# Softmax scores from two 12-bit float32r parts on four row tiles, with the maximum subtracted by a second matmul

## The reference

```
qkv = x @ qkv_w.T + qkv_b                       # x: 2048 x 128, normalised
q, k, v = split(qkv), 16 heads of 8
scores = einsum('bhqe,bhke->bhqk', q, k) / sqrt(8)
attn = softmax(scores, axis=-1)
out = einsum('bhqk,bhke->bhqe', attn, v)
out = out @ proj_w.T + proj_b
```

## Time and profile before

| | |
|---|---|
| median of the runs | 1883.54 us |
| the profiled execution's span | 1880.9 us |
| PE busy | 1635.9 us (87%), 7285 instructions |
| DVE busy | 1354.7 us (72%) |
| ACT busy | 836.9 us (44%) |
| POOL busy | 222.4 us (12%) |
| DMA moved | 29.49 MB |
| softmax attention, two passes | about 218 to 1036 us |

### The profile page before, as it was taken

One profiled execution on the slowest core, in us unless ns is written; L12 is line 12 of the kernel. 1 busy time (PEld: TensorE's weight loads), 2 busy tenths in 40 slices (PEclk: granted clock), 3 DMA queues, 4 the chain that ended last, 5 costly groups with the idle time before them and its releaser, 6 DMA issues. The chain is left out here.

```text
span 1880.9 us, 23731 instructions
## 1 busy us (share of the span) xinstructions
PE 1635.9 (87%) x7285; PEld 683.8 (36%) x7285; DVE 1354.7 (72%) x1951; ACT 836.9 (44%) x1493; POOL 222.4 (12%) x145
## 2 busy tenths in 40 slices
PE   6987589999999999999998798899994356589999
PEld 3433112222222222222221443366661122256665
DVE  5776788888888778888880577666656999745654
ACT  2433427777676666667778253322223000042222
POOL 2222300000000000000000022211101324301110
PEclk8998659999999999999999899899996777799999
DMA  6000400011001100111000000000000000000000
GB/s 168 2 0 1 135 16 8 14 27 40 9 14 28 30 12 7 27 30 24 2 2 2 1 1 0 1 1 0 0 1 0 0 0 1 0 1 6 6 5 7
DMA packets 32021, 29.49 MB, mean 16 GB/s; under 512 B 7788, under 2 KB 27032, under 8 KB 31928
## 3 DMA queue, kind: packets, MB, share of 16 engines
q1 hardware_dynamic: 31928, 28.31, 5.9%
HBM read 22.13 MB, written 4.19 MB: 14 GB/s over the span
## 5 line engine op out<-in xcount | busy, mean ns | idle before, releaser
L1382 DVE TENSOR_REDUCE mx<-ps 128x1 f32<-128x1024 f32 x512 | 605.2, 1220 | 147.5 <-PE ps L1269 143.2
L1269 PE MATMUL ps<-k,q 72*128 72x512 bf16 x1024 | 403.0, 408 | 11.4 <-DVE mx L1382 9.3
L1304 PE MATMUL ps<-q,k 84*128 84x512 bf16 x1024 | 346.8, 384 | 20.7 <-ACT xn L1359 14.5
L1359 ACT ACTIVATE xT<-ps 128x512 f32<-128x512 f32 x512 | 265.1, 603 | 156.7 <-PE ps L1304 156.6
L1359 ACT ACTIVATE xn<-ps 128x512 f32<-128x512 f32 x512 | 266.2, 603 | 107.4 <-PE ps L1304 107.4
L1269 PEld LDWEIGHTS ps<-k,q 72*128 72x128 bf16 x1024 | 110.1, 115 | 331.4 <-DVE mx L1382 185.4
L854 ACT ACTIVATE silu<-ps 128x512 f32<-128x512 f32 x144 | 85.3, 596 | 265.3 <-PE ps L827 261.9
L1304 PEld LDWEIGHTS ps<-q,k 84*128 84x128 bf16 x1024 | 102.3, 102 | 185.6 <-ACT xn L1359 69.6
L889 DVE TENSOR_TENSOR hid<-ps,silu 128x512 f32<-128x512 f32 x144 | 97.8, 690 | 91.2 <-PE ps L831 89.6
L827 PE MATMUL ps<-xT,ew 128*128 (+1 forms) x288 | 151.0, 606 | 6.5 <-PEq L1750 4.8
L817 PEld LDWEIGHTS ps<-ew,hid 128*128 128x128 f32 x1152 | 138.7, 192 | 30.6 <-issue 29.9
(11 more groups left out here) (239 smaller groups left out, 1688.9 us busy)
## 6 DMA issues: line engine op xcount, KB each, us to landing
k<-k_parts SPq DMA_DIRECT2D x90, 64.0 KB
q<-q_parts SPq DMA_DIRECT2D x144, 32.0 KB
k<-k_parts SPq DMA_DIRECT2D x108, 32.0 KB
ew<-in_L_ffn_w_dram SPq DMA_DIRECT2D x2, 1024.0 KB
wraw<-in_L_ffn_w_dram SPq DMA_DIRECT2D x3, 512.0 KB, 6.7
q_parts<-part SPq DMA_DIRECT2D x4, 384.0 KB, 5.3
k_parts<-part SPq DMA_DIRECT2D x4, 384.0 KB, 2.6
v<-values SPq DMA_DIRECT2D x8, 144.0 KB, 4.2
```

What stands on the lines that cost most here:

```text
L1269: mm = nc.tensor.matmul(m.ps[:, S1B[i % 4], :], queries, k1[:, h, kc * CHUNK:(kc + 1) * CHUNK], start=True, stop=True)
L1304: nc.tensor.matmul(m.ps[:, S2_BANK[s], :], k2[:, h, kt * P:(kt + 1) * P], q[:, qc, h, :], start=True, stop=True).then_inc(s2_ready, 1)
L1359: nc.scalar.activation(ex[kt % P_RING][:, h, :], m.ps[:, S2_BANK[s], :], ACT.Exp).then_inc(exped, 1)
L1382: nc.vector.reduce_max(mx[:, h, qt, kc:kc + 1], m.ps[:, 2 * (i % 2):2 * (i % 2) + 2, :], AX.XY)\
```

## The change

q and k are split into two parts of 12 significant bits each, both held as 32-bit values: DVE cuts off the low 12 bits (`HI_BITS`), POOL subtracts to get the rest. Scores are formed from them by float32r matmuls over 2 x 2 x 8 = 32 rows, one head on each of four row tiles of 32 rows (partitions 0, 32, 64 and 96), so that a tile q or k1 or k2 holds all four heads of a group in 128 partitions. The rows of k no longer hold ones; a second matmul, over two rows of `ones` against the two parts of the negated maximum (`neg_row`), accumulates into the same bank after the score.

The first pass issues two matmuls together, of heads 0 and 1 or 2 and 3, on two row tiles and into two banks; the DVE reduction then gives one maximum for each of two heads and not one over two banks. There are 32 such pairs a unit, over key blocks in the outer loop. The second pass forms scores 0 and 1, then subtracts both maxima, and the same for 2 and 3. Each load of q, k1 or k2 is four DMAs of 32 partitions (every fourth), in place of nine of eight; the maxima are eight DMAs of two by four runs in place of four. Parts in DRAM are float32, two of them. The first group's k1 and the first q also come directly from the part tile, not from DRAM. ACT's fill of the ones in k2 is gone, and DVE's split of the maximum has two steps in place of five.

```
+PARTS2 = 2
+ROW_TILE = 32
+ROW_BLOCKS = PARTS2 * PARTS2
+HI_BITS = -4096
...
-    dram_q = nc.dram_tensor("q_parts", [PARTS, D, T], BF16, kind="Internal").ap()
-    dram_k = nc.dram_tensor("k_parts", [PARTS, D, T], BF16, kind="Internal").ap()
+    dram_q = nc.dram_tensor("q_parts", [PARTS2, D, T], F32, kind="Internal").ap()
+    dram_k = nc.dram_tensor("k_parts", [PARTS2, D, T], F32, kind="Internal").ap()
...
-    q = m.sb("q", [ROWS_M, CHUNKS, GH, CHUNK], BF16, stack=kv_stack)
-    k1 = m.sb("k1", [ROWS, GH, T], BF16, stack=kv_stack)
-    neg_part = m.sb("neg_part", [P, TPC, 32], BF16, stack=kv_stack)
+    q = m.sb("q", [P, CHUNKS, CHUNK], F32R, stack=kv_stack)
+    k1 = m.sb("k1", [P, T], F32R, stack=kv_stack)
+    ones = m.sb("ones", [P, P], F32R, stack=kv_stack)
+    neg_part = m.sb("neg_part", [P, TPC, 32], stack=kv_stack)
...
+    def rows_of(tile, r):
+        return tile[r:P:ROW_BLOCKS, :].bitcast(F32)
...
+            def low_part(n):
+                pool.wait_ge(hi_ready, n + 1)
+                nc.gpsimd.tensor_tensor(part[:, n % PART_RING, 1, :], full[:, n % 2, :], part[:, n % PART_RING, 0, :],
+                                        ALU.subtract).then_inc(lo_ready, 1)
...
-                step(nc.vector.tensor_tensor(rest[:, :], full[:, n % 2, :], part[:, n % PART_RING, 0, :], ALU.subtract))
-                step(nc.vector.tensor_copy(part[:, n % PART_RING, 1, :], rest[:, :]))
-                nc.vector.tensor_tensor(part[:, n % PART_RING, 2, :], rest[:, :], part[:, n % PART_RING, 1, :], ALU.subtract)\
-                    .then_inc(parts_ready, 1)
-                dve.wait_ge(parts_ready, n + 1)
+                dve.wait_ge(f32_ready, n + 1)
+                part_free(dve, n)
+                nc.vector.tensor_scalar(part[:, n % PART_RING, 0, :].bitcast(I32), full[:, n % 2, :].bitcast(I32), HI_BITS,
+                                        None, ALU.bitwise_and).then_inc(hi_ready, 1)
...
+                if n < N_DIRECT:
+                    tile = q[:, 0, :] if s == 0 else k1[:, c * CHUNK:(c + 1) * CHUNK]
+                    for r in range(ROW_BLOCKS):
+                        i = r // PARTS2 if s == 0 else r % PARTS2
+                        sp.dma_start(rows_of(tile, r), part[0:GH * HD, slot, i, :]).then_inc(direct[slot], 16)
...
-        k2 = m.sb("k2", [ROWS_M, GH, T], BF16, stack=stack)
+        k2 = m.sb("k2", [P, T], F32R, stack=stack)
...
-        done = [max(0, (k + 1 - HOLE) * STEPS // (STEPS - HOLE)) for k in range(-1, STEPS)]
+        done = [max(0, (k + 1 - HOLE) * PAIRS // (STEPS - HOLE)) for k in range(-1, STEPS)]
...
+            for r in range(ROW_BLOCKS):
+                eng.dma_start(rows_of(q[:, qc, :], r),
+                              dram_q[r // PARTS2, bass.ts(g, GH * HD), qc * CHUNK:(qc + 1) * CHUNK]).then_inc(q_loaded[qc], 16)
...
                 for b in range(P // 32):
-                    rows = neg_turned[b * 32:b * 32 + PARTS * GH, :, :].rearrange("r j t -> r (j t)").unsqueeze(1)\
-                        .to_broadcast([PARTS * GH, GH, P])
-                    sp.dma_start(q[ROWS:ROWS_M, qc, :, b * P:(b + 1) * P], rows).then_inc(max_loaded, 16)
+                    for i in range(PARTS2):
+                        rows = slice(b * 32 + i * GH, b * 32 + (i + 1) * GH)
+                        sp.dma_start(neg_row[i:P:ROW_TILE, slot, b * P:(b + 1) * P].bitcast(F32),
+                                     neg_turned[rows, :, :].rearrange("h j t -> h (j t)")).then_inc(max_loaded, 16)
 
...
-                h, qt, kc = i // (TPC * CHUNKS), i // CHUNKS % TPC, i % CHUNKS
...
-                if i % 2 == 0 and not (isinstance(g, int) and g == 0 and qc == 0 and i < len(S1B)):
-                    pe.wait_ge(s1_used, (g * CHUNKS + qc) * PAIRS + (i // 2 - 1))
-                queries = q[0:ROWS, qc, h, :].rearrange("r (p t) -> r t p", t=TPC)[:, qt, :]
-                mm = nc.tensor.matmul(m.ps[:, S1B[i % 4], :], queries,
-                                      k1[:, h, kc * CHUNK:(kc + 1) * CHUNK], start=True, stop=True)
-                if i % 2 == 1:
-                    mm.then_inc(s1_ready, 1)
+                    pe.wait_ge(q_loaded[qc], DMAS_R * g)
+                if qc == 0 and i % (PAIRS // CHUNKS) == 0 and not (isinstance(g, int) and g == 0):
+                    pe.wait_ge(k1_loaded[kc], DMAS_R * g)
+                if not (isinstance(g, int) and g == 0 and qc == 0 and i < 2):
+                    pe.wait_ge(s1_used, (g * CHUNKS + qc) * PAIRS + (i - 1))
+                for h in (2 * pair, 2 * pair + 1):
+                    rows = slice(h * ROW_TILE, (h + 1) * ROW_TILE)
+                    queries = q[rows, qc, :].rearrange("r (p t) -> r t p", t=TPC)[:, qt, :]
+                    mm = nc.tensor.matmul(m.ps[:, S1B[h], :], queries, k1[rows, kc * CHUNK:(kc + 1) * CHUNK],
+                                          start=True, stop=True)
+                mm.then_inc(s1_ready, 1)
...
-                def score(s):
-                    kt, h = s // GH, s % GH
-                    if not (first and s < len(S2B)):
-                        pe.wait_ge(exped, u * STEPS + (s - S2_SINCE[s] + 1))
-                    nc.tensor.matmul(m.ps[:, S2_BANK[s], :], k2[:, h, kt * P:(kt + 1) * P], q[:, qc, h, :],
-                                     start=True, stop=True).then_inc(s2_ready, 1)
+                def score(steps):
+                    for s in steps:
+                        kt, h = s // GH, s % GH
+                        rows = slice(h * ROW_TILE, (h + 1) * ROW_TILE)
+                        if not (first and s < len(S2B)):
+                            pe.wait_ge(exped, u * STEPS + (s - S2_SINCE[s] + 1))
+                        nc.tensor.matmul(m.ps[:, S2_BANK[s], :], k2[rows, kt * P:(kt + 1) * P], q[rows, qc, :],
+                                         start=True, stop=False)
+                    for s in steps:
+                        h = s % GH
+                        rows = slice(h * ROW_TILE, h * ROW_TILE + PARTS2)
+                        nc.tensor.matmul(m.ps[:, S2_BANK[s], :], ones[rows, :], neg_row[rows, qc % 2, :],
+                                         start=False, stop=True).then_inc(s2_ready, 1)
                 pe.wait_ge(max_loaded, DMAS_M * (u + 1))
                 for kt in range(TILES):
                     if qc == 0 and kt % (TILES // 2) == 0:
-                        pe.wait_ge(k2_loaded[kt // (TILES // 2)], DMAS_K * (g + 1))
+                        pe.wait_ge(k2_loaded[kt // (TILES // 2)], DMAS_R * (g + 1))
                     s = kt * GH
-                    score(s)
-                    score(s + 1)
+                    score([s, s + 1])
                     ahead(s)
-                    score(s + 2)
                     ahead(s + 1)
-                    score(s + 3)
+                    score([s + 2, s + 3])
...
-            low = 64
-            nc.scalar.activation(k2[low:ROWS_M, :, :], own_row[low:ROWS_M, :].unsqueeze(2).to_broadcast([ROWS_M - low, GH, T]),
-                                 ACT.Copy).then_inc(ones_stored, 1)
...
-                    h, qt, kc = 2 * i // (TPC * CHUNKS), 2 * i // CHUNKS % TPC, i % (CHUNKS // 2)
-                    nc.vector.reduce_max(mx[:, h, qt, kc:kc + 1], m.ps[:, 2 * (i % 2):2 * (i % 2) + 2, :], AX.XY)\
+                    kc, qt, pair = i // (PAIRS // CHUNKS), i // 2 % TPC, i % 2
+                    nc.vector.reduce_max(mx[:, 2 * pair:2 * pair + 2, qt, kc], m.ps[:, 2 * pair:2 * pair + 2, :], AX.X)\
...
+                nc.vector.tensor_scalar(out[:, :, :, 0].bitcast(I32), neg[:, :, :].bitcast(I32), HI_BITS, None,
+                                        ALU.bitwise_and).then_inc(max_steps, 1)
+                dve.wait_ge(max_steps, u * 3 + 2)
+                nc.vector.tensor_tensor(out[:, :, :, 1], neg[:, :, :], out[:, :, :, 0], ALU.subtract).then_inc(max_steps, 1)
```

More of the change, by code:

```diff
@@ L6 @@
 BF16 = mybir.dt.bfloat16
+F32R = mybir.dt.float32r
+I32 = mybir.dt.int32
 ALU = mybir.AluOpType
@@ L964, in softmax_attention @@
+    proj, f32_ready, hi_ready, lo_ready = m.sem("proj"), m.sem("f32_ready"), m.sem("hi_ready"), m.sem("lo_ready")
+    parts_out, v_ready, preloaded = [m.sem(f"parts_out{i}") for i in range(PART_RING)], m.sem("v_ready"), m.sem("preloaded")
+    direct = [m.sem(f"direct{i}") for i in range(PART_RING)]
     sides = [(0, scale, dram_q), (1, 1.0, dram_k)]
     jobs = [(0, 0)] + [(1, c) for c in range(CHUNKS)] + [(0, c) for c in range(1, CHUNKS)]
+    N_DIRECT = 1 + CHUNKS
     with ExitStack() as stack:
@@ L968, in softmax_attention, with part_free @@
         full = m.sb("full" + tag, [P, 2, CHUNK], stack=stack)
-        rest = m.sb("rest" + tag, [P, CHUNK], stack=stack)
-        part = m.sb("part" + tag, [P, PART_RING, PARTS, CHUNK], BF16, stack=stack)
+        part = m.sb("part" + tag, [P, PART_RING, PARTS2, CHUNK], stack=stack)
         norm = Norm(m, stack, "norm", m.X, None, [6, 7])
         block = stack.enter_context(nc.Block())
+        def part_free(engine, n):
+            if n >= PART_RING:
```

(26 more changed lines are left out.)

99 lines of the change are left out of this document (26 added, 73 removed).

## The result

The changed kernel takes 2418.14 us (median of four, 2397.82 to 2448.39) against 1883.72: a ratio of 1.281 (95% interval 1.275 to 1.287), 534 us slower. 1910 was forecast, with 1868 to 2070 as the range. The profiled execution spans 2396.0 us.

The account below looks back on a forecast made before the run. The prediction took a loop of latencies through PE's in-order queue as the bound. It added +21 us for fifteen units, +7 for the last and -1 before the stage, about +27 on 1883.5: 1910 us, range 1868 to 2070.

Parts of the forecast that it names:

- the loop: Second pass, per key tile: score four, weighting, score one, exponential in PE's in-order queue bound the kernel, 2.90 us round.
- with the clock granted at 0.99: Attention stage, 264 to 1036 us of the profile before: PE's granted clock, read beside PE 97% busy.
- doesn't overlap: Rival: row tiles don't overlap, loop 3.70 us, +0.68 a tile for 240 tiles; 2060 us, chance 10%.
- the others: Remaining rivals: loads exposed 2010 us, 13%; float32r in two passes 2180 us, 8%; faster, second matmuls hidden, 1783 us, 14%.
- float32r: Score matmuls of the new type: taken at 0.22 us each, with 0.43 and more kept as a rival.
- The first-pass pair: First pass, two matmuls on different row tiles: 0.22 us in the loop instead of 0.46; other end 0.43.
- the forecast 3.13: Attention key tile in the changed kernel: sum of the loop's terms in us, against 3.02 before.
- The loads: Weight loads and draining of the array, per key tile: +0.06 us, ends -0.06 and +0.28.
- The second matmul: Maxima subtracted after each score: 0.22 + 0.22 us on the loop; last unit 2.38 becomes 2.38 + 0.44.
- SyncE: Issue of eight maxima DMAs for four: free at 2.9 us; upper end 2.7 us late a unit, +40.
- the stage before: Stage writing the parts ahead of attention: -1 us, ends -6 and +6.
- Weight loads on a busy tile: Rival: loads exposed at three successions on one tile in the loop, some +0.4 us a tile; 2010 us, chance 13%.

Follow-up runs that it names:

- pairs_before: Kernel before with the weighting moved ahead of score four and first-pass matmuls always issued two at a time, both of one pair of banks: 1857.9 us, ratio 0.986.
- pairs_only: Kernel before in its own order, weighting behind score four, with first-pass matmuls always issued two at a time: 1873.1 us, ratio 0.994.
- order_before: Kernel before with only the weighting moved ahead of the fourth score instead of behind it: 1912.8 us, ratio 1.016.
- fewrows: Kernel before with its 72-row score matmuls cut to 8 rows and its 84-row ones to 20; order, number and columns kept: 2455 us, ratio 1.305.
- fill2: Changed kernel plus two untiled 128-row bf16 matmuls a key tile ahead of score three, their results discarded: 2004.6 and 2069.1 us in two runs.
- fill2_bf16: Changed kernel with parts, ones and maxima in bfloat16, plus two untiled 128-row filler matmuls a key tile: 1901.6 us, ratio 1.010.
- fill2_contig: Changed kernel with two untiled fillers a key tile, first pass taking neighbouring queries instead of every fourth as stationary operand: 2009.8 and 2020.8 us.

## Why the prediction was wrong

**The bound before**: that a full PE was not it is shown, since pairs_before does the same matmuls in 1.4% less time. That the loop was it is supported and not proven. Its sum gave 2.81 for the tiles of pairs_only, and 2.81 was measured; but the gapless stream of pairs_before takes 2.82, so these tiles don't tell the loop from a full PE. order_before was the direct trial, and it went the other way, with tiles of 2.82 for 3.04 and others of 3.24 for 2.84.

**The step that failed** stands in the prediction's first paragraph: "with the clock granted at 0.99". The prediction read this as a property of the stretch and carried it over to other matmuls; no term, rival or bound held a clock of 0.5. It was a result of what PE did there, 72 and 84 rows a matmul. With 32 rows a tile and more gaps the clock went, and PE's terms of the loop nearly doubled: 0.98 to 1.83 for the weighting, tiles 3.05 and 3.40 to 4.95 and 5.40. fewrows shows what few rows do without any other change, fill2 shows the loss undone. The rival "doesn't overlap" and the others were no substitute: each of them slows some terms, the clock slows all of PE's.

**The size of its share.** fill2 at the full clock has 52.9 to 53.9 us a unit and 48.6 for the last, against 48.4 and 38.0 before: about 5 x 15 + 11 = 86 us slower, near 1970 (an estimate from these units). Of the 534 us, some 450 are the clock's. The 86 are still three times the 27 forecast: a size that was off, beside the step that failed.

**float32r** runs in one pass of 0.22 at the full clock, and row tiles overlap, pairs and even four: both as taken. The first-pass pair was one mis-sized term: 0.22 us, whether it stands behind scores three and four or behind the weighting. Behind the scores it costs nothing (score four to the weighting takes 0.66 with a pair and without one), which makes up for what the second matmuls took beyond their 0.22, so that the 3.05 near the forecast 3.13 is in part luck. Behind the weighting it costs 0.46, and the tile 3.40. The loads were the other: +0.06 us a tile, with +0.28 as the end. fill2 less fill2_bf16 gives 5.0 us a unit, 0.31 a tile, for the type as a whole. The prediction had priced the load as such (192 ns), not that of a stationary operand at a stride of 16 bytes (304), and only 0.12 of the 3.40 us hung on the stride.

**The second matmul** was priced right: 0.47 measured in the last unit, 0.44 forecast. "The prediction is wrong if the last unit's period doesn't grow": it grew, from 2.38 to 4.88 (in fill2, clock held and two fillers a tile, to 3.05; without the second matmuls it was 2.58 there). Of the 0.23 between this 3.05 and the forecast 2.82, fill2_bf16 has none: its last unit runs at 2.80.

**SyncE and the stage before** were right. The next stage starts at 216.5 us for 218.35, 1.9 earlier where 1 was forecast; eight maxima DMAs take 4.3 to 4.65 us to issue, where four took 3.3, and PE waits for them once, before unit 0 (2.3 us, and 2.2 in fill2).

**Weight loads on a busy tile.** The prediction's sign for exposed loads was a second matmul 0.3 us or more behind its score. Both cases occur. In the tile of 3.40 score one and the second matmul's load are both recorded at 285.80, on one row tile, and the second matmul follows at 286.03: 0.23 behind, the load hidden. In the tile of 3.05, where score one came just after the weighting, it is 0.33 behind, and behind score four 0.34. So loads can overlap matmuls on their own row tile, and still 0.11 or 0.12 us show at some of the steps. That rival's mechanism was right in part, and its 2010 us lies near the full-clock 1970; against the measured 2418 either says nothing.

## What to carry to other kernels

A granted clock in a profile belongs to the matmuls that ran there. Before matmuls are narrowed to fewer rows or packed into row tiles, price the stage at both clocks; if PE works near the edge, a few wide matmuls in its idle slots may buy back far more than they cost. And where two engines hand over a double buffer, keep both halves of a pair together in the in-order queue: that alone made the kernel before 0.6% faster, and 1.4% with the weighting moved ahead of score four.

## What the runs showed of the hardware

- PE at the lower level while 99.7% busy (548.6 of 550 us, 8 and 20 rows a matmul); at the upper one (0.99) with the same stream over 72 and 84 rows.
- Matmuls on different row tiles start out of program order. In the tile above, a first-pass pair (300.10) starts ahead of the second matmul of score four (300.43), which stands before it in the queue and waits for its own row tile. The first-pass pair at 298.69 likewise is ahead of 299.01.
- A float32r weight load of 128 columns took 191 to 203 ns with neighbouring elements and 304 with every fourth one, a bfloat16 one 109 with every fourth.
- After the pause of PE at a loop branch, kernels near the edge ran half a unit or more at the lower clock: 73.4 us for 53.9 in fill2, 88.3 for 53.2 in fill2_contig, 69.1 for 49.1 in fill2_bf16, while the kernel before lost some 5.6 us.
